# Step 0's key and query rows written directly, the first steps reordered, and the key blocks of steps 1 to 3 shared out anew

## What is computed

```python
q, k, v = heads(ln(x) @ Wq + bq), heads(ln(x) @ Wk + bk), heads(ln(x) @ Wv + bv)
y = softmax(where(causal, q @ k.T * scale, -inf)) @ v
y = y + softmax(qc @ kc.T * scale) @ vc          # kc, vc from the context
x = x + (merge(y) @ Wp + bp)
h = ln(x)
w = top8(sigmoid(h @ Wr + br)), normalised
x = x + shared(h) + sum_e w[e] * ((silu(h @ Wg[e] + bg[e]) * (h @ Wu[e] + bu[e])) @ Wd[e] + bd[e])
```

## Time and profile before

| what | before |
|---|---|
| median of 3 runs | 197.84 us |
| profiled execution | 198.4 us |
| its span | 196.7 us |
| TensorE busy | 187.0 us (95%) |
| VectorE, ScalarE, GpSimd busy | 149.3, 137.8, 111.8 us |
| first product of step 0 / step 1 / step 2 | 14.83 / 20.21 / 24.38 us |
| mean granted TensorE clock | 0.995 of full speed |

### The profile page before, as it was taken

How to read it: one execution, slowest core, us unless ns; L and a number is a source line. 1 busy time by engine, 2 the same in 40 slices (tenths; PEclk the granted TensorE clock), 3 DMA queues, 4 the chain that set the end, 5 groups by cost and what they waited for, 6 DMA issues and landing times.

```text
span 196.7 us, 4006 instructions
## 1 busy us (share of the span) xinstructions
PE 187.0 (95%) x1254; PEld 138.9 (71%) x1254; DVE 149.3 (76%) x343; ACT 137.8 (70%) x280; POOL 111.8 (57%) x181
## 2 busy tenths in 40 slices
PE   7979979999999999998999999999999999999992
PEld 2536757778777767775776788688788888888671
DVE  2998997767667765898664779779777888887982
ACT  3546878799789887988788763975655556555471
POOL 6989995546397699947936468696622333000020
PEclk9999999999999999999999999999999999999997
DMA  4354422322234232510221203031000000000003
GB/s 113 103 139 131 116 75 68 76 69 68 70 97 101 65 87 63 131 33 3 66 54 36 49 0 76 8 79 24 0 0 3 0 0 0 0 2 3 0 0 107
DMA packets 20434, 10.40 MB, mean 53 GB/s; under 512 B 11881, under 2 KB 18542, under 8 KB 20414
## 3 DMA queue, kind: packets, MB, share of 16 engines
q1 hardware_dynamic: 19290, 9.24, 18.6%
q0 software_dynamic: 672, 0.69, 1.4%
q10 hardware_dynamic: 452, 0.23, 0.5%
HBM read 4.51 MB, written 0.52 MB: 26 GB/s over the span
## 4 chain that ended last, share of the span: by engine, by line
PE 64%; DVE 11%; POOL 11%; issue 5%; DMA 3%; ACT 3%; DVEq 0%; POOLq 0%; ACTq 0%
PE psum L1756 10%; PE psum L1421 7%; PE psum L1422 7%; PE psum L1423 7%; POOL hid_lo L740 4%; PE psum L1615 4%; PE psum L1603 4%; PE psum L1578 4%; PE psum L1522 4%; PE psum L1625 3%; PE psum L1751 3%; PE psum L1583 3%; PE psum L1521 3%; POOL ckey_rows L458 2%; POOL key_rows L444 2%
## 5 line engine op out<-in xcount | busy, mean ns | idle before, releaser
L983 ACT ACTIVATE gate<-psum,bias_cols 128x512 f32<-128x512 f32 (+2 forms) x35 | 23.5, 675 | 23.9 <-PE psum L1423 23.9
L845 ACT ACTIVATE probs<-psum 128x512 f32<-128x512 f32 x64 | 36.3, 596 | 2.3 <-PE psum L1583 1.2
L740 POOL TENSOR_TENSOR hid_lo<-hid,hid_hi 128x512 fp32r<-128x512 f32 x13 | 16.8, 1291 | 29.3 <-ACT hid_hi L992 29.2
L1365 DVE SCALAR_TENSOR_TENSOR gated<-psum,bias_cols,gate 128x512 f32<-128x512 f32 x32 | 23.9, 748 | 10.0 <-ACT gate L983 10.0
L1522 PE MATMUL psum<-key_blocks,query_rows 96*128 96x512 f32 x48 | 24.1, 545 | 0.0
L1377 DVE TENSOR_TENSOR hid<-gated,psum 128x512 f32<-128x512 f32 x32 | 21.9, 683 | 1.9 <-PE psum L1751 0.3
L659 POOL TENSOR_TENSOR w_late_lo<-w_ffn,w_late_hi 128x384 fp32r<-128x384 f32 x11 | 12.8, 1163 | 18.0 <-ACT w_late_hi L857 18.0
L992 ACT CAST hid_hi<-hid 128x512 fp32r<-128x512 f32 (+1 forms) x33 | 20.2, 613 | 2.5 <-DVE hid L1377 1.6
L1146 DVE TENSOR_REDUCE row_max<-psum 128x4 fp32r<-128x512 f32 x16 | 11.0, 689 | 13.9 <-PE psum L1522 13.8
L1150 DVE TENSOR_REDUCE row_max<-psum 128x4 fp32r<-128x1024 f32 x16 | 19.4, 1214 | 0.0
L1421 PE MATMUL psum<-xT_hi,w_late_hi 128*128 128x512 f32 x42 | 16.8, 399 | 0.1
(11 more groups left out here) (208 smaller groups left out, 516.6 us busy)
## 6 DMA issues: line engine op xcount, KB each, us to landing
query_rows<-queries SPq DMA_DIRECT2D x46, 64.0 KB, 2.1
key_rows<-keys SPq DMA_DIRECT2D x39, 32.0 KB, 1.9
w_ffn<-in_L_ffn_Wg SPq DMA_DIRECT2D x16, 64.0 KB, 2.0
w_ffn<-in_L_ffn_Wu SPq DMA_DIRECT2D x16, 64.0 KB, 2.2
w_ffn<-in_L_ffn_Wd SPq DMA_DIRECT2D x16, 64.0 KB, 2.1
ckey_rows<-ckeys POOLq DMA_DIRECT2D x12, 32.0 KB, 2.1
key_rows<-keys POOLq DMA_DIRECT2D x9, 32.0 KB, 2.2
x_sb<-in_x SPq DMA_DIRECT2D x2, 128.0 KB, 2.8
```

The costliest lines, as they stand in the source:

```text
L740: pool.tensor_tensor(hid_lo[:, n % 3, :], hid[:, n % 3, :], hid_hi[:, n % 3, :].bitcast(F32), ALU.subtract).then_inc(pool_lo_done, 1)
L845: act.activation(probs[:, i % 2, c, :], bank(B_ST + c % 2), ACT.Exp, scale=SCALE).then_inc(exp_done, 1)
L983: act.activation(gate[rows_of(n), n % 3, part], psum[of, B_GATE + n % 2, part], ACT.Silu, bias=bias_cols[of, BIAS_GATE + u:BIAS_GATE + u + ...
L1365: dve.scalar_tensor_tensor(out=gated[:, n % 3, :], in0=bank(B_UP + n % 2), scalar=bias_cols[:, BIAS_UP + u:BIAS_UP + u + 1], in1=gate[:, n ...
```

## The change

Step 0's rows of keys, queries and cross queries no longer pass through DMAs. The weights' first 32 columns are laid out three times (`tripled`), so that three extra products (`project_direct`) give all 96 rows at once; ScalarE writes them rounded to their place (`round_direct`) and VectorE overwrites the third that holds the remainder (`split_direct`). Group 0 has its own mask and row order. Step 0's maxima are turned in two halves (`first_turn`, `first_shift`), and its scores begin inside `natural(0)`. Batch 1's values, and the context's values, move from before step 0's scores to the tail of step 1; `x_pair` moves to step 2, `keys_queries` to 3 and 5, `cross_values` to 4 and 6, `y_turn` of batch 0 behind step 6's attention, `route_turn` of batch 0 from the end of step 12 to right behind `natural(14)`.

ScalarE makes all four key blocks of steps 1 and 2 (`ACT_ALONE`), VectorE two each of steps 0, 3 and 4. GpSimd makes all context blocks, batch 0's as one product a group, the other batches' later, in steps 0 to 3. It also issues step 1's query rows; SyncE issues the rest of batch 0's key and query rows, and GpSimd no key rows. The values' bias is added at `y_turn` instead of to the values. Fillers: 28 instead of 33, four each ahead of `turn_max(1)` and `turn_max(2)`.

The core of the diff (removed lines mostly left out):

```diff
...
+ACT_ALONE = (1, 2)
...
-        for b in range(FIRST_BATCHES, BATCH):
-            tail_at[2 * b - 3] = [("keys_queries", b)]
-            tail_at[2 * b - 2] = [("cross_values", b)]
-        late_at = {}
+        tail_at = {1: [("values", 1)]}
+        for b in range(2, BATCH):
+            tail_at[2 * b - 1] = [("keys_queries", b)]
+            tail_at[2 * b] = [("cross_values", b)]
...
+                if (name, b) != ("y_turn", 0):
+                    tail_at.setdefault(4 * b + 6 + n, []).append((name, b))
             between_at[4 * b + 8] = [("norm", b)]
-        late_at[12] = [("route_turn", 0)]
...
+        def queries_of(b, g):
+            if (b, g) == (0, 0):
+                return direct_split, 2
+            if (b, g) == (0, 1):
+                return pool_placed_q, 48
+            return placed_q[b % 2][g], placements(b, g) - 48 * (b == 2 and g == 1)
...
+        def act_heads(i):
+            return range(GROUP) if i in ACT_ALONE else (2, 3)
+        def act_blocks(i):
+            return a_blocks_set, sum(len(act_heads(k)) for k in range(i + 1))
...
+            if i in ACT_ALONE:
+                return act_blocks(i)
             if i < POOL_BLOCKS:
-                return v_blocks_set, 2 * i + 2
+                return v_blocks_set, 2 * sum(k not in ACT_ALONE for k in range(i + 1))
             return pool_blocks_set, 2 * (i - POOL_BLOCKS) + 2
...
+            sp.wait_ge(ckey_rows_set, 1)
+            sp.wait_ge(ck_rounded, 1)
+            place_ctx_keys(sp, 0, (0, 1))
+            sp.wait_ge(ck_split, 1)
+            place_ctx_keys(sp, 0, (2,))
             sp.wait_ge(qkc_rounded, 1)
-            place_keys(sp, 0, 0, (0, 1))
+            place_keys(sp, 0, 1, (0, 1))
             sp.wait_ge(qkc_split, 1)
-            place_keys(sp, 0, 0, (2,))
+            place_keys(sp, 0, 1, (2,))
+            place_keys(sp, 0, 2)
             sp.wait_ge(qkc_split, 3)
-            place_queries(sp, 0, 0, (1,))
-            for g in range(1, GROUPS):
-                place_queries(sp, 0, g)
+            place_queries(sp, 0, 2)
+            place_keys(sp, 0, 3)
...
+            pool.wait_ge(w_qkv_rounded, 2)
+            pool.tensor_tensor(w_qkv_lo[:, 2:4, :], w_qkv[:, 2:4, :], w_qkv_hi[:, 2:4, :].bitcast(F32),
+                               ALU.subtract).then_inc(pool_w_split, 1)
+            pool.wait_ge(w_direct_rounded, 2)
+            pool.tensor_tensor(tripled(w_direct_lo, slice(2, 3)), first_group(w_qkv, slice(2, 3)),
+                               tripled(w_direct_hi, slice(2, 3)).bitcast(F32), ALU.subtract).then_inc(pool_w_split, 1)
             first_rstd(1)
+            pool.wait_ge(ckey_rows_set, 1)
             pool.wait_ge(ck_rounded, 1)
             pool.wait_ge(ck_split, 1)
+            place_ctx_keys(pool, 1)
+            pool.wait_ge(qkc_rounded, 3)
+            place_queries(pool, 0, 1, (0, 2))
+            place_ctx_keys(pool, 2, (0,))
...
+            def first_ctx(g):
+                pool.wait_ge(placed_ck[g], 48)
+                spread_ctx(g, slice(0, 1), first_ckeys_set)
+            def later_ctx(g):
+                spread_ctx(g, slice(1, BATCH), later_ckeys_set)
+                pool.wait_ge(later_ckeys_set, g + 1)
...
+            first_ctx(0)
+            place_ctx_keys(pool, 2, (1, 2))
+            pool.wait_ge(qkc_split, 3)
+            place_queries(pool, 0, 1, (1,))
+            first_ctx(1)
+            place_ctx_keys(pool, 3)
+            pool.wait_ge(first_ckeys_set, 2)
+            pool.memset(cvalue[:, :, :, :], 0.0).then_inc(zeroed, 1)
+            pool.wait_ge(zeroed, 2)
...
+            first_ctx(2)
+            pool.wait_ge(first_ckeys_set, 3)
...
+                if i == 0:
+                    first_ctx(3)
+                    pool.wait_ge(first_ckeys_set, GROUPS)
+                if i == 1:
+                    first_rstd(2)
+                if i < GROUPS:
+                    later_ctx(i)
...
+            def round_direct(k):
+                to = (key_rows[0:SHIFT_ROW, 0, 0, :], query_rows[0:SHIFT_ROW, 0, 0, 0, :],
+                      query_rows[0:SHIFT_ROW, 0, 0, 1, :])[k]
+                bias = ORDER[k][1] + BIAS_DIRECT
+                act.wait_ge(m_direct, k + 1)
+                if k == 0:
+                    act.wait_ge(rows_set, 1)
+                act.activation(to, psum[0:SHIFT_ROW, B_DIRECT[k], 0:SEQ], ACT.Identity,
+                               bias=bias_cols[0:SHIFT_ROW, bias:bias + 1]).then_inc(direct_rounded, 1)
...
+            act.wait_ge(have_bias_cols, 1)
+            act.wait_ge(m_ck, 1)
+            act.activation(ckeys[:, 0, :], bank(B_CK, CTX_KEYS), ACT.Identity,
+                           bias=bias_cols[:, BIAS_CK:BIAS_CK + 1]).then_inc(ck_rounded, 1)
+            round_direct(0)
+            round_direct(1)
+            round_qkc(0, 0)
+            expand(0)
+            round_qkc(0, 1)
+            round_qkc(0, 2)
+            round_direct(2)
             def shift(i):
...
+            def first_shift(s):
+                act.wait_ge(t_max, s + 1)
+                act.copy(query_rows[SHIFT_ROW:ROWS, 0, 0, s, :],
...
+            round_x(1)
+            first_shift(0)
+            expand(1)
+            act.wait_ge(m_v, 1)
+            act.wait_ge(zeroed, 1)
+            act.copy(value[:, 0:2, :, 0:D],
+                     value_bank(0).rearrange("p (t h d) -> p t h d", t=2, h=HEADS)).then_inc(have_value, 1)
+            exps(0, (0,))
+            first_shift(1)
+            exps(0, (1,))
             expand(2)
-            act.wait_ge(have_neg_mean, 1)
-            norm(4)
-            norm(5)
+            round_qkc(1, 0)
+            shift(1)
             exps(0, (2, 3))
-            shift(1)
-            norm(6)
-            norm(7)
+            expand(3)
+            round_qkc(1, 1)
+            round_qkc(1, 2)
             for i in range(STEPS - 2):
                 if i:
...
+                if i == 12:
+                    tail("route_turn", 0)
...
+            dve.wait_ge(in_x[1], 16)
+            measure(x_sb, slice(*NORM_GROUPS[1]))
             norm(0)
...
+            dve.wait_ge(w_direct_rounded, 1)
+            dve.tensor_tensor(tripled(w_direct_lo, slice(0, 2)), first_group(w_qkv, slice(0, 2)),
+                              tripled(w_direct_hi, slice(0, 2)).bitcast(F32), ALU.subtract).then_inc(w_direct_split, 1)
+            spread_of(slice(*NORM_GROUPS[1]), var_ready)
...
+            def split_direct(k):
+                part = (KEY_PARTS, QUERY_PARTS, QUERY_PARTS)[k].index(1)
+                rows = slice(PART * part, PART * (part + 1))
+                to = (key_rows[rows, 0, 0, :], query_rows[rows, 0, 0, 0, :], query_rows[rows, 0, 0, 1, :])[k]
+                bias = ORDER[k][1] + BIAS_DIRECT
+                dve.wait_ge(direct_rounded, k + 1)
...
+            split_direct(0)
+            split_direct(1)
+            dve.wait_ge(rows_set, 1)
+            dve.wait_ge(have_mask, 1)
+            expand(0)
+            negative_mean(1)
+            split_qkc(0, 0)
...
                     tile_1()
-                    values(1)
+                    split_qkc(0, 1)
+                    split_qkc(0, 2)
+                    split_direct(2)
+                    split_x(1)
+                    dve.wait_ge(t_ffn_bias, 1)
+                    dve.tensor_copy(bias_cols[:, 0:LATE_BIAS_ROWS],
...
+            expand(3)
             for i in range(STEPS):
-                if i + 3 < POOL_BLOCKS:
-                    expand(i + 3)
+                if i == 2:
+                    negative_mean(2)
                 if i + 2 < STEPS:
                     maxima(i + 2, i - 2)
+                if i == 0:
+                    for n in range(3):
+                        split_qkc(1, n)
                 if i == STEPS - 2:
...
                         tail_rest(name, b)
+                if i == 1:
+                    expand(4)
+                    stats_of(2)
...
+            def project_direct(k):
+                tensor = ORDER[k][0]
+                product3(psum[0:SHIFT_ROW, B_DIRECT[k], 0:SEQ], w_direct_hi[:, tensor, :], w_direct_lo[:, tensor, :],
+                         xT_hi[:, tokens(0)], xT_lo[:, tokens(0)]).then_inc(m_direct, 1)
...
+            run_idle(1, B_OUT)
+            pe.wait_ge(xT_split, 1)
+            pe.wait_ge(w_direct_split, 1)
+            project_direct(0)
+            project_direct(1)
+            pe.wait_ge(w_qkv_split, 1)
+            project_qkc(0, 0)
+            project_qkc(0, 1)
+            pe.wait_ge(pool_w_split, 1)
             project_qkc(0, 2)
-            project_values(0)
-            run_idle(7, B_NAT0)
-            turn_x(1)
...
-            run_idle(5, B_NAT0)
+            pe.wait_ge(direct_split, 1)
+            pe.wait_ge(pool_w_split, 2)
+            project_direct(2)
+            pe.wait_ge(have_bias_cols, 1)
+            run_idle(2, B_NAT1)
...
+                if i == 1:
+                    pe.wait_ge(max_done, 2)
+                elif i:
...
+                    pe.wait_ge(qkc_split, 1)
```

(62 more changed lines are left out.)

388 lines of the change are left out of this document (182 added, 206 removed).

## The result

The kernel after takes 198.59 us, the median of 10 runs (198.10 to 199.17), against 197.85 us of the kernel before in as many runs: 1.0037 times as long, 95% interval 1.0019 to 1.0055. The change makes it slower by 0.37%, and the prediction, 196.6 us and faster, was wrong.

A forecast was written before the change was run, and what follows sets the result against it. TensorE, full from 30 us on, bounds the kernel, so only the first 30 us can gain: lead 3.3 - 1.9 put off = 1.4, - 0.15 = 1.25 us; 197.84 - 1.25 = 196.6 us, range 195.0 to 198.3.

The forecast's parts named there:

- Step 0: Start without row DMAs: `natural(0)` at 10.4 us, 4.4 earlier, and `scores(0, 0)` at 13.9.
- step 1: `natural(1)` at 17.0 us, 3.2 earlier, set by the last query DMA, issued at 14.8 and landing 2.2 later.
- step 2: `natural(2)` at 20.6 us, 3.8 earlier, where the limits of ScalarE's blocks and VectorE's maxima meet; added fillers cost nothing.
- what is late next: Batch 1's row DMAs begin at 24.0 us; ScalarE waits 1.9, `natural(4)` at 30.7, `scores(3, 0)` at 35.3, then 0.3 more waiting.
- The lead of 3.3 us: TensorE's lead at `scores(3, 0)` against 38.86 in the kernel before: 3.56 - 0.3 = 3.3 us.
- Put off: Work left for after `scores(3, 0)`, `keys_queries` of batch 2 and `cross_values`: 1.9 us off the lead, leaving 1.4.
- `y_turn`, -0.15: On the ending chain, one VectorE addition with bias, 0.48 for 0.42 us, at two or three places: 0.15 us lost.
- Route turn, 0: Moving it from step 12 gains 0, bounds 0 and 0.86 us, as `natural(15)` stays behind GpSimd's blocks.
- B: GpSimd's queue is late, so late query rows delay `natural(1)` and eat the gain: 197.5 to 198.2 us; chance 0.17.
- C: Batch 1's rows, split behind `maxima(2)`, become the limit: slower, above 198.2 and up to 199.5 us; chance 0.13.
- D: ScalarE feeds the direct rows late, `natural(0)` at 12 us: 197.4 to 198.2 us; chance 0.05.
- A: More of the lead stays, 2.5 to 3.2 us: 194.6 to 195.3 us; chance 0.17.

The follow-up runs named there:

- before, again: The kernel before, run again unchanged: 197.71 us against 197.65, ratio 1.0015; its profiled execution took 197.54 us with a span of 195.8.

## Why the prediction was wrong

**Step 0, step 1, step 2 and what is late next: right, the first 0.55 us optimistic.** 10.95, 17.02, 20.75, 30.88, 35.86 for 10.4, 17.0, 20.6, 30.7, 35.3, ScalarE's wait 1.75 for 1.9. That 17.0 came out is partly luck: TensorE was forecast to be free at 16.4 and the query rows to land at 17.0, but TensorE itself was busy with batch 1's projections until 17.02. (From the rows named there, the last query DMA's issue comes out at 14.0 to 14.6, not at 14.8; it ran from 14.58 to 15.08.) Behind step 3 there was no wait of 0.3 us: from step 3 to step 4 the kernel after took 5.47 us, before 5.48. Ahead of it there was one of 0.56, in front of attention 1 at 34.12, and not for ScalarE, whose load the forecast had counted. By its code this attention waits for `normalized`, and VectorE's `o_norm` ends 0.1 us before it, at 34.02, although the trace puts the wait down to no engine. With 35.86 against 35.3 + 0.3, the start gave 0.3 us less than forecast.

**The lead of 3.3 us: the step that failed.** It was read against 38.86, the mark of an execution 0.6 us behind the usual one (median 38.27). The prediction knew that the median lay 0.56 us below that execution, and subtracted it at the end as if it had nothing to do with the change. But it was made in the very stretch that the change replaces, in front of step 3, where VectorE's blocks had taken 1.48 us and TensorE waited 0.70 us for the maxima behind them. So the same loss was counted twice, once as gained and once as not there. The lead of the usual execution was 2.40: 0.6 of the missing 0.9 is this mark, 0.3 the start. This is the largest single error in a miss of 2.0 us, and it would not alone have turned a gain into a loss; the terms that were put at nothing (step 15, the expert stage, the time outside the span) did the rest.

**Put off, 1.9: right.** From step 3 to step 7 the kernel after takes 1.87 us longer in five of seven traces.

**`y_turn`, -0.15: right in size.** From step 7 to step 12 the kernel after loses 0.18 us. TensorE has a gap of 0.16 us at 68.01, in front of attention 7. Like attention 1 it starts 0.1 us behind VectorE's `o_norm`, which ends at 67.90 here and at 68.00 in "before, again", where TensorE's lead is 0.30 us at step 8. So VectorE's lead of 0.1 us counts there; that the new `y_turn` is behind it is not shown.

**Route turn, 0: right in its reason.** `natural(15)` stayed behind GpSimd's blocks. What was missed is that those blocks do not follow TensorE's lead; 0.33 us are lost from step 12 to step 14. The bound of 0.86 us is real, 1.1 us, once the blocks move too.

**Not in the sum at all:** 0.34 us in the expert stage, two thirds of it by the tiles' places; 0.22 outside the span, most of it by ScalarE's program; up to 0.36 by the loads behind SyncE's row DMAs, a queue that "What is late next" had followed for its rows alone.

**The balance:** 2.40 - 1.87 - 0.18 - 0.33 leaves a lead of nothing at step 14 (0.02); minus 0.34 in the expert stage the span is 0.3 us longer, and up to 0.7 where the loads are late. With 0.22 outside that makes 0.5 to 0.9 us. Measured are 0.6 in the spans and 0.74 to 0.95 in the times.

**The rivals.** None was right. B named the mechanism that decides the start (VectorE slowed beside GpSimd), but the change avoids it: where it was put back it cost 1.2 us in the median. C named the right side, slower, but not the reason: batch 1's rows began at 24.4, as forecast, and `natural(4)` at 30.88. D did not occur. A asked for more lead than there was. The Trainium skill's page "SBUF — State Buffer", section "SBUF: two separate sides", was weighed as speaking against the change. Here 2.61 us instead of 0.62 beside GpSimd's memset and DMA issue agree with its exclusive lock, though no run shows the lock by itself; the rule speaks for `ACT_ALONE`. That GpSimd's DMAs are held up too is not seen: three issues took 1.52 us beside the slow blocks and 1.47 to 1.71 in the kernel before.

## What to carry to other kernels

Before a gain is worked out against a mark, see whether the profiled execution is a usual one, and if it is not, in which stretch it lost: a correction by the median may take back what the change removes. Several traces of each kernel, compared stretch by stretch, agree here to some hundredths and give each term of the sum its size. Where the trace names no engine for a wait, read in the code what the instruction waits for. When an engine's own work is brought forward, follow each chain of other engines that ends in it (here norm, masks, split, key blocks) up to the end of the kernel; the lead is worth only what the latest of them allows. An edit that adds tiles or instructions can cost some tenths of a microsecond far from where it acts, so look also at identical products in an untouched stage and at the time outside the span.

## What the runs showed that was not expected

- Products of the same shape, 128x512 at full clock, took 399 or 404 ns, and 390 or 395 ns, by where the tiles lie (1856 bytes further or not): 0.22 and 0.25 us in some 78.
- Fifteen more instructions on ScalarE, all waits long satisfied, brought a last transfer of instructions behind the end of the span and 0.15 us; twelve more on GpSimd or six on SyncE did not.
- VectorE's pair of 100x256 blocks took 0.61 us beside GpSimd's DMA issue, 1.01 and 1.48 beside its context products, and 2.61 beside DMA issue and a memset.
- Two executions of one kernel differ by 0.85 us made in the first 38 us and then kept to a hundredth or two until the end.
